# Projections after three graph layers: the normalisation of each pair of tiles moved from VectorE to ScalarE

## The chip, the cores and the metric

The kernel runs on one core of one Trainium2 chip. The metric is the time of one execution on the device in microseconds, the median of several runs. In the text PE is TensorE (matmuls; PEld its weight loads), DVE is VectorE, ACT is ScalarE, POOL is GpSimd and SP is SyncE, which here only issues DMAs.

## The reference

3125 nodes with 128 features and 53125 edges, sorted by destination. Four graph layers follow each other, each added to its input and normalised:

```python
def _layernorm(x, axis=-1, eps=1e-05):
    m = jnp.mean(x, axis=axis, keepdims=True)
    v = jnp.var(x, axis=axis, keepdims=True)
    return (x - m) / jnp.sqrt(v + eps)
...
    x = _layernorm(x + _L0_gnn_ref(x, edge_index, edge_type_16, ...), axis=-1)
    x = _layernorm(x + _L1_gnn_ref(x, src, dst, edge_type_32, ...), axis=-1)
    x = _layernorm(x + _L2_gnn_ref(x, edge_index, L2_gnn_W, L2_gnn_b), axis=-1)
    x = _layernorm(x + _L3_gnn_ref(x, ..., src, dst), axis=-1)
```

The first two layers sum messages of typed edges. The third is `relu(agg @ W.T + b)`, with `agg` the plain sum of the neighbours' rows. The fourth is an attention over the edges with 8 heads, whose queries, keys and values are `x @ Wq + bq` (times 0.25), `x @ Wk + bk` and `x @ Wv + bv`.

## The kernel before, in words

The nodes are 25 tiles of 128 rows. The program has five stages: the three sums over edges (`sums_body` for L[0], L[1] and L[2]), the projections (`post_body` in `sum_layers`), and the attention (`attention`). Each engine runs a stage's instructions in an order written out by hand; between stages all meet (`pass_end`, and `pass_close` on DVE).

The change is in the projections alone. They take the aggregated, transposed rows of the third layer (`aggT`), finish that layer, and make queries, keys and values. The tiles go in pairs: `DUOS` is 13, pair u holds tiles 2u and 2u+1, and the last pair has one tile. For pair u, in the order of the data:

- PE multiplies by the third layer's weights (`last_product`, L970) into `p_g`.
- DVE (`last_front`) adds the bias (L1703), takes relu and adds the layer's input (L1706), and takes mean and variance of each tile (bn_stats L1709, bn_aggr L1713) into `mv`.
- ACT takes the square root of variance plus eps for both tiles in one instruction (`deviations`, L1079) into `std`.
- DVE (`last_back`) takes the reciprocal (L1720) into `rstd` and normalises each tile, `(y - mean) * rstd`, with one tensor_scalar (L1724). The tiles land in `XA`, or in the half of `XH` that a register (`aside`, read by a value_load) names. This raises `s_done`.
- PE transposes both tiles (`last_transposed`, L979), and ACT copies them out of PSUM into `H` (`last_copy`, L1084).
- PE multiplies them by the weights of keys and values (L997); DVE adds the bias (`keys_values`, L1733), and SP stores the result to `kv_d` (L697).

The order on each engine, for u from 0 on: PE does `last_product(u + 1)`, `keys_values(u - 1)`, `last_transposed(u)`, and from u = 3 on one `table_rows` (L987). DVE does `last_front(u)`, `keys_values(u - 2)`, `last_back(u)`, and for u from 1 to 7 one of the `row_tables` (L1674 to L1691). ACT does `deviations(u)`, `last_copy(u)`, then two wipes of the attention's buffers (L1090) and, for u from 3 to 11, one `chunk_tables` (L1097), which reads what `table_rows` made. The wipes and tables are for the attention; nothing in this stage reads them. POOL prepares the tables' input beside the first five pairs or so (L740, L742) and then waits until all keys and values are stored, before it starts the attention's gathers (L1950).

After the last pair PE makes the queries (`queries`, L1007), DVE and ACT split each into three bfloat16 parts (L1741, L1748, L1103), and SP stores them to `q_d` (L700). Then the attention starts.

Of the kernel before, what the change touches and what calls it, by code (L numbers as in the profile page):

```python
# [11 lines left out]
ALU = mybir.AluOpType  # L12
ACT = mybir.ActivationFunctionType
AX_X = mybir.AxisListType.X

P = 128
# [3 lines left out]
NT = 25  # L20
# [290 lines left out]
def sum_layers(nc, ctx, a, d, con, dst_s, base4, n_f, ns_i, np_i, XH, idx, shared, cont, s_arr):  # L311
    def sb(name, shape, dt=F32):
        return ctx.enter_context(nc.sbuf_tensor(name, shape, dt))
# [4 lines left out]
    def sem(name):  # L318
        return ctx.enter_context(nc.semaphore(name))
# [42 lines left out]
    y = sb("y", [P, 4, D])  # L362
    bn6 = sb("bn6", [P, 4, 6])
    mv = sb("mv", [P, 4, 2])
    std = sb("std", [P, 4, 1])
    rstd = sb("rstd", [P, 4, 1])
    kv_s = sb("kv_s", [P, 3, 2, 2 * D])
    work = sb("work", [P, NT * SLAB // 2 + OHS * (KEYS + P) // 2])
    XA, H = XH[:, 0:NT], XH[:, NT:2 * NT]
# [108 lines left out]
    s_y0, s_y, s_bs, s_ba, s_std, s_rs, s_done = (sem(f"s_{k}") for k in ("y0", "y", "bs", "ba", "std", "rs", "done"))  # L478
# [552 lines left out]
    def scalar(act, wiped):  # L1031
        act.dma_start(con[:], a["con"]).then_inc(s_con, 16)
        act.dma_start(lim, a["lim"]).then_inc(s_lim, 16)
        for w, name in ((w_self, "w_self"), (w_bases, "w_bases"), (w_basis, "w_basis"), (w_loop, "w_loop"),
# [7 lines left out]
                       scale=0.0).then_inc(s_clr, 1)  # L1042
# [30 lines left out]
        def deviations(u):  # L1073
            n = min(2, NT - 2 * u)
            two = slice(u % 2 * 2, u % 2 * 2 + n)
            act.wait_ge(s_ba, u + 1)
            if u >= 2:
                act.wait_ge(s_rs, u - 1)
            act.activation(std[:, two, 0], mv[:, two, 1], ACT.Sqrt, bias=con[:, C_EPS:C_EPS + 1], scale=1.0).then_inc(s_std, 1)  # L1079

        def last_copy(u):
            n = min(2, NT - 2 * u)
            act.wait_ge(s_xtr, u + 1)
            act.activation(H[:, 2 * u:2 * u + n, :].rearrange("p t d -> p (t d)"), p_xt[:, 0:n * D],  # L1084
                           ACT.Copy).then_inc(s_xtc, 1)

        def wipe(k):
            for ap in wiped:
                n = ap.shape[1]
                act.activation(ap[:, k * n // DUOS:(k + 1) * n // DUOS],  # L1090
                               bc(con[:, C_ONE:C_ONE + 1], 2, (k + 1) * n // DUOS - k * n // DUOS)[:, 0], ACT.Copy,
                               scale=0.0).then_inc(s_wipe, 1)

        def chunk_tables(n):
            ks = slice(n * TK, min((n + 1) * TK, KB))
            act.wait_ge(s_wide, n + 1)
            act.activation(pen[:, ks], p_o[:, 0:(ks.stop - ks.start) * (P + 1)].rearrange("p (k e) -> p k e", e=P + 1),  # L1097
                           ACT.Copy, scale=LOW).then_inc(s_pen, 1)

        def part(g, k):  # L1100
            tiles = slice(g * QG, min((g + 1) * QG, NT))
            act.wait_ge(s_q[2 * k], g + 1)
            act.activation(q_p[:, tiles, k, :], q_f[:, g % 3, 0:tiles.stop - tiles.start, :],  # L1103
                           ACT.Copy).then_inc(s_q[2 * k + 1], 1)
# [104 lines left out]
        def post_body():  # L1209
            act.wait_ge(s_ball, 32)  # L1210
            act.activation(b_q, b_q, ACT.Copy, scale=float(HD) ** -0.5).then_inc(s_bq, 1)
            for u in range(DUOS):
                deviations(u)
                last_copy(u)
                wipe(u)
                if 0 <= u - 3 < TPARTS:
                    chunk_tables(u - 3)
            for i in range(QGROUPS + 2):
                for k in range(3):
                    if 0 <= i - k < QGROUPS:  # L1220
                        part(i - k, k)
# [3 lines left out]
                       scale=0.0).then_inc(s_clr, 1)  # L1225
# [5 lines left out]
    def vector(dve):  # L1231
# [440 lines left out]
        def row_tables(n):  # L1672
            if n == 0:
                dve.memset(shared[0:1, T_ROW:T_TAB], LOW)  # L1674
                dve.wait_ge(s_rows, 48)
                ins = dve.tensor_tensor(cont[:], bends[:, 0], bends[:, 1], ALU.is_equal)
            elif n == 1:
                ins = dve.tensor_tensor(eq_r[:, 0], ends[:, 0, 0:EC], ends[:, 0, 1:EC + 1], ALU.is_equal)
            elif n == 2:
                ins = dve.tensor_tensor(eq_r[:, 1], ends[:, 1, 0:EC], ends[:, 1, 1:EC + 1], ALU.is_equal)  # L1680
            elif n == 3:
                ins = dve.tensor_tensor(eq_f, ends[:, 1, 0:EC:CB], ends[:, 1, CB:EC + 1:CB], ALU.is_equal)
            elif n == 4:
                dve.wait_ge(s_row, 4)
                ins = dve.tensor_scalar(pen_r[:, :, 0, 1:CB + 1], eq_r[:, 0].rearrange("p (k c) -> p k c", c=CB), -1.0,
                                        -LOW, ALU.add, ALU.mult)
            elif n == 5:
                ins = dve.tensor_scalar(pen_r[:, :, 1, 0:CB], eq_r[:, 1].rearrange("p (k c) -> p k c", c=CB), -1.0,
                                        -LOW, ALU.add, ALU.mult)
            else:  # L1690
                ins = dve.tensor_scalar(pen_f[:, :, 0:KB], bc(eq_f, 1, HEADS), -1.0, -LOW, ALU.add, ALU.mult)  # L1691
            ins.then_inc(s_row, 1)

        def last_front(u):
            if u == 0:
                dve.wait_ge(s_ball, 32)
            n = min(2, NT - 2 * u)
            two = slice(u % 2 * 2, u % 2 * 2 + n)
            tiles = slice(2 * u, 2 * u + n)
            dve.wait_ge(s_o, u + 1)  # L1700
            if u >= 2:
                dve.wait_ge(s_done, u - 1)
            dve.tensor_tensor(y[:, two, :], p_g[:, u % 3, 0:n * D].rearrange("p (t d) -> p t d", d=D), bc(b_lin, 1, n),  # L1703
                              ALU.add).then_inc(s_y0, 1)
            dve.wait_ge(s_y0, u + 1)
            dve.scalar_tensor_tensor(y[:, two, :], y[:, two, :], 0.0, XA[:, tiles, :], ALU.max, ALU.add).then_inc(s_y, 1)  # L1706
            dve.wait_ge(s_y, u + 1)
            for j in range(n):
                last = dve.bn_stats(bn6[:, two.start + j, :], y[:, two.start + j, :])  # L1709
            last.then_inc(s_bs, 1)  # L1710
            dve.wait_ge(s_bs, u + 1)
            for j in range(n):
                last = dve.bn_aggr(mv[:, two.start + j, :], bn6[:, two.start + j, :])  # L1713
            last.then_inc(s_ba, 1)

        def last_back(u, aside):
            n = min(2, NT - 2 * u)
            two = slice(u % 2 * 2, u % 2 * 2 + n)
            dve.wait_ge(s_std, u + 1)
            dve.reciprocal(rstd[:, two, :], std[:, two, :]).then_inc(s_rs, 1)  # L1720
            dve.wait_ge(s_rs, u + 1)
            for j in range(n):
                t, k = 2 * u + j, two.start + j
                last = dve.tensor_scalar(XH[:, t:t + NT + 1, :][:, bass.ds(aside, 1), :].rearrange("p a d -> p (a d)"),  # L1724
                                         y[:, k, :], mv[:, k, 0:1], rstd[:, k, :], ALU.subtract, ALU.mult)
            last.then_inc(s_done, 1)

        def keys_values(u):
            n = min(2, NT - 2 * u)
            dve.wait_ge(s_pkv, u + 1)  # L1730
            if u >= 3:
                dve.wait_ge(s_kvst[u % 3], 16 * (u // 3))
            dve.tensor_tensor(kv_s[:, u % 3, 0:n, :], p_d[:, u % 3, 0:n * 2 * D].rearrange("p (t d) -> p t d", t=n),  # L1733
                              bc(b_kv, 1, n), ALU.add).then_inc(s_kv, 1)
# [9 lines left out]
        def rest(g, k):  # L1744
            n = min(QG, NT - g * QG)
            dve.wait_ge(s_q[2 * k - 1], g + 1)
            part = q_f[:, g % 3, 0:n, :]
            dve.tensor_tensor(part, part, q_p[:, g * QG:g * QG + n, k - 1, :], ALU.subtract).then_inc(s_q[2 * k], 1)  # L1748

        def post_body():  # L1750
            aside = dve.value_load(np_i[0:1, 2:3], min_val=0, max_val=NT)
            for u in range(DUOS + 2):
                if u < DUOS:
                    last_front(u)
                if 0 <= u - 2:
                    keys_values(u - 2)
                if u < DUOS:
                    last_back(u, aside)
                if 1 <= u < 8:
                    row_tables(u - 1)  # L1760
            dve.wait_ge(s_bq, 1)
            for i in range(QGROUPS + 2):
                if i < QGROUPS:
                    scaled(i)
                for k in (1, 2):
                    if 0 <= i - k < QGROUPS:
                        rest(i - k, k)
# [670 lines left out]
```

## Time and profile before

| | us |
|---|---|
| three runs | 2503.83, 2506.83, 2515.24 |
| median | 2506.83 |
| the profiled execution | 2512.79 |
| its span | 2511.0 |

Busy in the span: PE 1715.0 us (68%), PE's weight loads 1376.8 (55%), DVE 1502.9 (60%), POOL 1425.4 (57%), ACT 1127.2 (45%). The granted clock of TensorE has a mean of 0.698 of full speed.

Times in the profile count from the start of the span. A row of the timeline gives the start, the time from the first start to the last end of the instructions in it, the engine, the line, and in brackets how long the engine had been idle and what ended that. Instructions of one engine can overlap a little, so one may start before the one ahead of it ends. The line numbers are those of the kernel before.

### The profile page before, as it was taken

The numbers are of one execution on the slowest core, as the hardware profiler recorded it, in microseconds if no ns is written. First come the engines' busy times: TensorE is split into PE (matmuls) and PEld (weight loads), VectorE is DVE, ScalarE is ACT, GpSimd is POOL, SyncE is SP. The second block draws the span as 40 slices with busy tenths as digits, with TensorE's granted clock in tenths as the row PEclk, the third lists the DMA queues.
The fourth block names the chain that finished last, engine by engine and source line by source line (L and its number), as shares of the span: only waits on it lengthen the run. The fifth ranks groups of instructions, "written<-read, shape, count | busy, mean of one in ns | idle before, by whom it ended". The sixth has DMA issues, their size and how long they took to land.

```text
span 2511.0 us, 36111 instructions
## 1 busy us (share of the span) xinstructions
PE 1715.0 (68%) x10160; PEld 1376.8 (55%) x10160; DVE 1502.9 (60%) x4761; ACT 1127.2 (45%) x2223; POOL 1425.4 (57%) x1482
## 2 busy tenths in 40 slices
PE   2668777777478888884688898986135455564566
PEld 1556656656367666663666666754034454454456
DVE  5556555555467776774366666667345565665666
ACT  2235435545566666664245444534433432433433
POOL 6666666665466666653566666602756455555540
PEclk9655555555688999887789999998555555555555
DMA  5121221212123332323333333312644344443430
GB/s 152 47 75 48 73 74 49 73 48 70 44 80 87 87 114 61 111 81 103 87 87 88 111 90 113 111 64 67 175 133 122 112 132 119 120 130 117 119 114 6
DMA packets 171436, 231.76 MB, mean 92 GB/s; under 512 B 48220, under 2 KB 123983, under 8 KB 170980
## 3 DMA queue, kind: packets, MB, share of 16 engines
q0 software_dynamic: 53376, 123.02, 18.0%
q1 hardware_dynamic: 116710, 104.76, 13.8%
q10 hardware_dynamic: 1154, 1.67, 0.2%
q8 instruction: 86, 1.41, 0.2%
q14 instruction: 110, 0.90, 0.1%
HBM read 196.52 MB, written 36.08 MB: 93 GB/s over the span
## 4 chain that ended last, share of the span: by engine, by line
PE 20%; another core or an unknown queue 16%; ACT 10%; issue 8%; DVE 7%; SPq 2%; DMA 1%; DVEq 0%; ACTq 0%
PE p_d L918 4%; PE p_d L847 4%; PE p_g L905 3%; PE p_g L795 3%; ACT oht L2071 2%; PE p_o L828 1%; ACT oht L2077 1%; PE p_d L807 1%; ACT L2118 1%; PE p_w L2005 1%; ACT late L1122 1%; ACT L2102 1%; DVE Sb L1399 1%; SPq L1915 1%
## 5 line engine op out<-in xcount | busy, mean ns | idle before, releaser
L728 POOL DMA_INDIRECT G<-h_d,idx x624 | 615.9, 987 | 402.1 <-issue 159.4
L1950 POOL DMA_INDIRECT G<-kv_d,idx x416 | 394.5, 948 | 325.1 <-DVE PV L2256 173.8
L728 POOL DMA_INDIRECT G<-in_x,idx x416 | 400.6, 963 | 217.1 <-issue 106.8
L795 PEld LDWEIGHTS p_g<-S,G 128*128 128x128 f32 x2080 | 376.4, 245 | 225.7 <-issue 184.8
L795 PE MATMUL p_g<-S,G 128*128 128x96 f32 (+1 forms) x2080 | 398.3, 325 | 147.4 <-issue 145.2
L1391 DVE TENSOR_TENSOR agg<-agg,p_g 128x96 f32 (+1 forms) x520 | 120.6, 232 | 338.0 <-remote 194.0
L918 PE MATMUL p_d<-Sb,kv_s 128*128 128x288 f32 x728 | 245.1, 458 | 77.4 <-ACT kv_s L1135 57.6
L1482 DVE TENSOR_TENSOR work<-work,p_d 128x312 f32 (+1 forms) x416 | 180.4, 465 | 145.5 <-remote 77.3
L1364 DVE SCALAR_TENSOR_TENSOR S<-con,rel,shared 128x96 f32<-128x96 f32 (+1 forms) x1040 | 262.1, 294 | 0.4 <-issue 0.2
L1143 ACT ACTIVATE work<-con,lo_f 128x128 bf16<-128x128 f32 x416 | 143.1, 392 | 234.0 <-remote 114.8
L807 PE MATMUL p_d<-work 128*128 128x312 bf16 (+1 forms) x832 | 198.6, 368 | 55.1 <-issue 35.0
L2005 PE MATMUL p_w<-oh,PV 128*128 128x40 f32 x832 | 195.1, 410 | 26.0 <-DVE PV L2256 25.1
L2005 PEld LDWEIGHTS p_w<-oh,PV 128*128 128x128 f32 x832 | 187.6, 330 | 33.4 <-DVE PV L2256 28.1
L918 PEld LDWEIGHTS p_d<-Sb,kv_s 128*128 128x128 f32 x728 | 136.7, 210 | 113.8 <-ACT kv_s L1135 62.1
L1399 DVE SCALAR_TENSOR_TENSOR Sb<-con,slots 128x288 f32<-128x288 f32 x364 | 174.3, 513 | 17.2 <-remote 9.4
L1135 ACT ACTIVATE kv_s<-p_g 128x512 f32<-128x512 f32 (+1 forms) x104 | 56.2, 540 | 246.4 <-remote 160.3
L2081 ACT ACTIVATE R<-p_sm 1x128 f32<-1x128 f32 x26 | 6.9, 266 | 328.9 <-remote 306.8
L807 PEld LDWEIGHTS p_d<-work 128*128 128x128 bf16 x832 | 99.9, 134 | 98.5 <-issue 74.2
L1468 DVE TENSOR_SCALAR work<-iota_h,key_f 128x600 bf16<-128x600 f16 x416 | 153.9, 380 | 0.0
L2228 DVE TENSOR_TENSOR_SCAN R<-pen_b,R 1x136 f32<-1x136 f32 x26 | 11.1, 428 | 204.3 <-ACT R L2082 194.6
L847 PE MATMUL p_d<-work,q_s 128*128 128x512 bf16 (+1 forms) x525 | 125.4, 379 | 6.3 <-DMA work<-A_d 4.6
L905 PE MATMUL p_g<-XH,hot 128*128 128x128 f32 x728 | 95.0, 284 | 46.1 <-ACT hot L1128 46.1
(315 smaller groups left out, 3179.5 us busy)
## 6 DMA issues: line engine op xcount, KB each, us to landing
dst_b<-in_dst_row SPq DMA_DIRECT2D x104, 240.0 KB
work<-A_d SPq DMA_DIRECT2D x25, 800.0 KB
A_d<-work SPq DMA_DIRECT2D x12, 1600.0 KB
G<-h_d,idx POOLq DMA_INDIRECT x624
G<-in_x,idx POOLq DMA_INDIRECT x416
kv_s<-low_d SPq DMA_DIRECT2D x52, 128.0 KB
G<-kv_d,idx POOLq DMA_INDIRECT x416
kv_s<-low_d SPq DMA_DIRECT2D x52, 96.0 KB
```

Of the source, the lines that this page charges most:

```text
L728: pool.indirect_dma_start(G[:, n % GRING, :], None, l.table, bass.IndirectOffsetOnAxis(ap=l.places[:, c:c + 1], axis=0)).then_inc(s_arr[i ...
L795: last = pe.matmul(p_g[:, g % PB, 0:width], G[:, c % GRING, :], S[:, c % (SRING * GR), 0:width], start=(k == 0), stop=(k == GR - 1))
L807: last = pe.matmul(p_d[:, 1 + half, 0:(hi - lo) * W], lows[:, slot, :], keys[:, slot, lo * W:hi * W], start=(k == 0), stop=(k == GR - 1))
L847: last = pe.matmul(p_d[:, 1 + n % 2, 0:width], q_s[:, t % QS, k, :], A_s[:, t % AB, cols], start=(t == two[0] and k == 0), stop=(t == two[ ...
L905: last = pe.matmul(p_x[:, k * P:(k + 1) * P], hots[n % 2][:, t % 2, k, :], l.x_in[:, t, :], start=(t == tiles[0]), stop=(t == tiles[-1]))
L918: pe.matmul(p_s[:, 0:l.nb * WB], picked[:, n % 2, at:at + P], Sb[:, m % SBR, 0:l.nb * WB], start=(k == 0), stop=(k == GRP - 1)).then_inc(s ...
L1364: last = dve.scalar_tensor_tensor(S[:, slot + k, 0:l.nb * W].rearrange("p (b w) -> p b w", w=W), bc(iota, 1, l.nb), rel[:, c:c + 1], bc(co ...
L1399: dve.scalar_tensor_tensor(Sb[:, m % SBR, 0:l.nb * WB].rearrange("p (b w) -> p b w", w=WB), bc(con[:, C_I + 1:C_I + 1 + WB], 1, l.nb), row ...
L1468: dve.tensor_scalar(keys[:, slot, :], iota_h[:], key_f[:, c:c + 1], None, ALU.is_equal).then_inc(s_hot, 1)
L1482: dve.tensor_tensor(place, place, p_d[:, 1 + half, 0:(hi - lo) * W].rearrange("p (t w) -> p t w", w=W), ALU.add).then_inc(s_bad, 1)
L1950: pool.indirect_dma_start(G[:, c % KRING, :], None, d["kv"], bass.IndirectOffsetOnAxis(ap=idx[:, c:c + 1], axis=0)).then_inc(s_arr[c // QC ...
L2005: pe.matmul(p_w[:, q % 2, 0:WA], PV[:, q % VRING, c, :], oh1[:, k % OH1, j * QC + c, :], start=(c == 0), stop=(c == QC - 1))
```

## The change: what it does

The tensor_scalar on DVE is replaced by an ACTIVATE (Identity, which gives scale * x + bias) on ACT for each tile, with `rstd` as scale and `shift` as bias, where `shift` is minus mean times `rstd`. DVE makes `shift` for both tiles of a pair with one scalar_tensor_tensor behind the reciprocal. Both raise `s_rs`, so its counts double. The reciprocal, which overwrites what ACT reads as scale, gets a wait on `s_done`. The value_load of `aside` moves from DVE to ACT, behind the scaling of `b_q` (L1211).

```diff
     rstd = sb("rstd", [P, 4, 1])
+    shift = sb("shift", [P, 4, 1])
...
             if u >= 2:
-                act.wait_ge(s_rs, u - 1)
+                act.wait_ge(s_rs, 2 * (u - 1))
             act.activation(std[:, two, 0], mv[:, two, 1], ACT.Sqrt, bias=con[:, C_EPS:C_EPS + 1], scale=1.0).then_inc(s_std, 1)
+
+        def normalised(u, aside):
+            n = min(2, NT - 2 * u)
+            act.wait_ge(s_rs, 2 * (u + 1))
+            for j in range(n):
+                t, k = 2 * u + j, u % 2 * 2 + j
+                last = act.activation(XH[:, t:t + NT + 1, :][:, bass.ds(aside, 1), :].rearrange("p a d -> p (a d)"),
+                                      y[:, k, :], ACT.Identity, bias=shift[:, k, :], scale=rstd[:, k, :])
+            last.then_inc(s_done, 1)
...
             act.activation(b_q, b_q, ACT.Copy, scale=float(HD) ** -0.5).then_inc(s_bq, 1)
+            aside = act.value_load(np_i[0:1, 2:3], min_val=0, max_val=NT)
             for u in range(DUOS):
                 deviations(u)
+                normalised(u, aside)
                 last_copy(u)
...
-        def last_back(u, aside):
+        def last_back(u):
             n = min(2, NT - 2 * u)
             two = slice(u % 2 * 2, u % 2 * 2 + n)
             dve.wait_ge(s_std, u + 1)
+            if u >= 2:
+                dve.wait_ge(s_done, u - 1)
             dve.reciprocal(rstd[:, two, :], std[:, two, :]).then_inc(s_rs, 1)
-            dve.wait_ge(s_rs, u + 1)
-            for j in range(n):
-                t, k = 2 * u + j, two.start + j
-                last = dve.tensor_scalar(XH[:, t:t + NT + 1, :][:, bass.ds(aside, 1), :].rearrange("p a d -> p (a d)"),
-                                         y[:, k, :], mv[:, k, 0:1], rstd[:, k, :], ALU.subtract, ALU.mult)
-            last.then_inc(s_done, 1)
+            dve.wait_ge(s_rs, 2 * u + 1)
+            dve.scalar_tensor_tensor(shift[:, two, 0], mv[:, two, 0], -1.0, rstd[:, two, 0], ALU.mult,
+                                     ALU.mult).then_inc(s_rs, 1)
...
         def post_body():
-            aside = dve.value_load(np_i[0:1, 2:3], min_val=0, max_val=NT)
...
-                    last_back(u, aside)
+                    last_back(u)
```

## Rows read from the trace of the kernel before

**Rows 1.** The head of the page.

```profile
span 2511.0 us, 36111 instructions
```

**Rows 2.** Busy by window: us, PE, PEld, DVE, ACT, POOL, clock, DMA share, GB/s.

```profile
1707.30:1711.20 3.90, 3.29 (x10) 2.39 (x10) 3.25 (x10) 1.46 (x4) 3.69 (x6) 0.50 0.00 0
...
1726.20:1745.60 19.40, 13.08 (x64) 8.30 (x64) 17.44 (x64) 10.55 (x30) 0.00 (x0) 1.00 0.24 83
1745.60:1748.50 2.90, 2.58 (x7) 1.33 (x7) 2.06 (x7) 1.65 (x5) 0.00 (x0) 0.69 0.31 112
```

**Rows 3.** The timeline, pair 9 and the start of pair 10.

```profile
1737.88 0.29 ACT L1079 ACTIVATE std<-mv,con 128x2 f32<-128x2 f32 x1
1738.20 0.17 DVE L1720 RECIPROCAL rstd<-std 128x2 f32<-128x2 f32 x1
1738.51 0.60 DVE L1724 TENSOR_SCALAR XH<-y,mv,rstd 128x128 f32 x2
1739.03 0.42 DVE L1703 TENSOR_TENSOR y<-p_g,late 128x256 f32<-128x256 f32 x1
...
1739.17 0.44 PE L979 MATMUL p_xt<-con,XH 128*128 128x128 f32 x2 [1.02 <-DVE XH L1724]
...
1739.64 0.38 ACT L1084 ACTIVATE XH<-p_xt 128x256 f32<-128x256 f32 x1 [1.48 <-PE p_xt L979]
...
1739.92 0.61 ACT L1090 ACTIVATE agg<-con 128x499 f32<-128x499 f32 x1
...
1740.43 0.41 ACT L1090 ACTIVATE SC<-con 128x256 f32<-128x256 f32 x1
...
1740.74 0.48 ACT L1097 ACTIVATE shared<-p_o 128x387 f32<-128x387 f32 x1
1741.11 0.29 ACT L1079 ACTIVATE std<-mv,con 128x2 f32<-128x2 f32 x1
1741.44 0.17 DVE L1720 RECIPROCAL rstd<-std 128x2 f32<-128x2 f32 x1 [0.15 <-ACT std L1079]
```

**Rows 4.** The timeline, the first three pairs.

```profile
1704.12 0.31 ACT L1211 ACTIVATE late<-late 128x128 f32<-128x128 f32 x1 [27.58 <-DMA late<-in_w_qkv]
...
1705.84 0.30 ACT L1079 ACTIVATE std<-mv,con 128x2 f32<-128x2 f32 x1 [1.41 <-DVE mv L1713]
...
1709.93 1.23 DVE L1724 TENSOR_SCALAR XH<-y,mv,rstd 128x128 f32 x2
...
1711.21 0.69 PE L979 MATMUL p_xt<-con,XH 128*128 128x128 f32 x2 [0.51 <-DVE XH L1724]
1711.33 0.97 DVE L1674 MEMSET shared<- 1x1100 f32 x1 [0.17 <-issue]
...
1714.76 0.98 DVE L1724 TENSOR_SCALAR XH<-y,mv,rstd 128x128 f32 x2
```

**Rows 5.** Groups by line and form: busy us, mean ns, idle before.

```profile
L1167 ACT ACTIVATE hot<-con,kv_s 128x128 f32<-128x128 f32 x208 | 63.3, 386 | 37.7 <-remote 36.3 <-PE p_g L881 1.4
...
L1064 ACT ACTIVATE act_r<-p_o,now 128x128 f32<-128x128 f32 x25 | 9.0, 361 | 0.0
...
L1063 ACT ACTIVATE act_o<-p_o 128x128 f32<-128x128 f32 x25 | 6.9, 277 | 37.1 <-remote 26.1 <-PE p_o L832 7.0 <-issue 3.8
...
L1568 DVE SCALAR_TENSOR_TENSOR now<-now,npf,itc 128x1 f32<-128x1 f32 x2 | 0.4, 200 | 0.0
```

**Rows 6.** Waits from 1750 to 1800 us: us in total, times, longest.

```profile
DVE cur L2165 <- issue: 2.1, 1, 2.1
```

**Rows 7.** The timeline of ACT in the third sum.

```profile
1618.42 1.28 ACT L1070 ACT_TABLE_LOAD   x1
...
1623.79 1.32 ACT L1122 ACTIVATE hot<-kv_s,con 128x512 f32<-128x512 bf16 x2
```

**Rows 8.** The timeline, transposes of the last two pairs.

```profile
1745.64 0.44 PE L979 MATMUL p_xt<-con,XH 128*128 128x128 f32 x2 [1.19 <-DVE XH L1724]
...
1748.51 0.48 PE L979 MATMUL p_xt<-con,XH 128*128 128x128 f32 x1
```

## The prediction

> **What bounds the kernel now.** I read four views in this order. The head of the profile gives the span, 2511.0 us [rows 1]; the same execution took 2512.79 us, so 1.8 us lie around the span, and it stands 6 us above the median of the three runs, 2506.83. The sum below is a difference, so I set it against 2512.79 and carry it over to the median unchanged. The busy time by window shows where the change lives: the projections run from 1704 to about 1751 us, some 47 us or 1.9% of the span, and within 1726.2 to 1745.6 no engine is full: DVE 17.44 of 19.40 us, PE 13.08, ACT 10.55 [rows 2]. No single engine's sum therefore gives the answer; the loop of waits does.
>
> That loop is in the timeline of one steady pair [rows 3]. ACT takes the square root of pair 9 (L1079) at 1737.88, DVE's reciprocal starts at 1738.20, DVE's normalisation at 1738.51, PE's transposes at 1739.17, ACT's copy out of PSUM (L1084) at 1739.64; then ACT does work which nobody in this stage waits for, two wipes (1739.92 and 1740.43) and one table (1740.74), and only then, at 1741.11, the square root of pair 10. That is 3.23 us, and each step starts on the end of the one before it. ACT is idle in it for 1.48 us, but its order is fixed, so the square root of the next pair can't pass the wipes. DVE runs nearly as long: it idles only 0.15 us, at 1741.44, where the reciprocal waits for the square root [rows 3]. So two loops are almost equal, and ACT's is ahead by that 0.15 us.
>
> **The change, part by part.**
>
> Removed from DVE: 25 normalisations. In the steady pairs two of them take 0.60 us and hold DVE's queue 0.52 us (1738.51 to 1739.03) [rows 3]. In the first pairs they cost more: 1.23 us for pair 1 and 0.98 for pair 2 [rows 4], where POOL is busy 3.69 of 3.90 us [rows 2]; from the start of pair 1's to DVE's next instruction 1.40 us go by [rows 4].
>
> Added to DVE: 13 small operations for the bias. The nearest row is a scalar_tensor_tensor on 128x1, 200 ns [rows 5]. The reciprocal's start to its dependant's start is 0.31 us now [rows 3] and stays, with the small operation in the dependant's place. ACT then starts on its end, so 0.20 us is new in the loop. Bounds: 0.16, if it costs what the reciprocal does (0.17 less a rounding), and 0.3.
>
> Added to ACT: 25 ACTIVATEs on 128x128, scale and bias both from SBUF. No row has both. With a pointer for the bias, 128x128 f32 takes 386 ns; a pointer for the scale is worth 361 - 277 = 84 ns, from the two ACTIVATEs on the same PSUM tile [rows 5]. I take 470 ns. Consecutive ACTIVATEs overlap by 0.10 us (1739.92 + 0.61 against 1740.43) [rows 3], so a pair takes 0.94 - 0.10 = 0.84 us, against 0.60 on DVE: 0.24 us more in the loop. Bounds: 0.07, if the second pointer is free (2 x 386 - 100 = 672 ns), and 0.34 with no overlap. The output's address comes from a register, as it did on DVE, and I see no gap for it there: I price it at nothing.
>
> Moved in the queues: on ACT the normalisation stands between square root and copy. What waits behind it is this pair's copy, which needs the transposes of this very data anyway, then wipes, table and the next square root. So nothing can use ACT's wait for DVE's two small operations, as nothing could before. On DVE, the next front (L1703) and the keys and values (L1733) now start as soon as the bias is out, 0.52 us sooner; they end earlier and DVE waits for the square root instead. The added wait on s_done before the reciprocal is for a normalisation two pairs back, long over. DMAs are neither added nor moved.
>
> So a steady pair gets 0.20 + 0.24 = 0.44 us longer, 3.23 to 3.67. The steps stay alike to the end: from pair 9's transposes at 1739.17 [rows 3] to pair 11's at 1745.64 [rows 8] it is 6.47 us for two. From the transposes of pair 4 to those of pair 11 there are seven such steps: **+3.1 us**. The last pair has one tile: + 0.20 and 0.47 against 0.35: **+0.3 us**.
>
> The first four pairs go the other way. There ACT has no table to do (0.30 us less), and DVE has a memset of 0.97 us [rows 4] and row tables on top, so DVE is the late one at pairs 2 and 3. Walking these pairs with the durations above (normalisation gone from DVE, bias added, 0.84 us on ACT) gives, as an estimate, the transposes of pairs 0 to 4 at +0.2, +0.1, -0.4, -0.5 and -0.2 us against now; ACT's loop catches up as soon as its tables begin. I take **-0.2 us** for the lot, with bounds of -1.5 (all of DVE's relief stays) and +0.5.
>
> The value_load moved to ACT sits between the scaling of b_q and the first square root. The only bound from a row is DVE's 2.1 us of issue ahead of L2165, where a value_load and more stand [rows 6]. ACT has 1.4 us between these two now (1704.12 + 0.31 to 1705.84) [rows 4], so it costs 0 to 0.7 us once; I take 0.1.
>
> What follows the stage starts from its end: the queries, which PE has in its queue behind the last keys and values, the 25 stores of q, and the attention, which reads what they store; POOL's gathers wait for the last store of keys and values. I take the delay as passed on whole; nothing ahead of the attention has slack to swallow it, though a loop as long as the attention's could give or take a little.
>
> Sum: 3.1 + 0.3 - 0.2 + 0.1 = **+3.3 us**. The profiled execution would be 2516.1, the median 2510.1 us. About 0.5% (12.5 us) is what a measurement can tell from no change here, and this is a quarter of it.
>
> **The clock, weighed.** From 1719.4 to 1745.6 the granted clock is 1.00, the 2.4 GHz level, with PE busy 67% of the time; in the first pairs it is 0.50, the 1.2 GHz level, and it falls again after 1745.6, to a mean of 0.69 [rows 2]. In my sum it stays at 1.00. The Trainium skill, TensorE: Matmul & The Clock Gate, Part 1, says that the clock follows how busy PE has been recently; with pairs of 3.67 us the same work is 59% of the time, so by that rule the fall may come sooner. That is the first rival.
>
> **Rivals.**
>
> 1. *The clock falls within the steady pairs.* The transposes of a pair took 0.69 us at 0.50 (pair 1) and 0.44 at 1.00 [rows 3, 4]. So 0.25 us for some eight pairs: 2.0 us more, +5.3 in all, 2512.1. For it: the fall after 1745.6 came at no great loss of activity. Against: the stretch before held for 26 us. 15%.
>
> 2. *DVE was the loop that counted, and ACT's is shorter than I think.* If the wipes overlapped the waits, only DVE's relief would remain: 0.52 - 0.20 = 0.32 us per pair, times 13: -4.2 us, 2502.6. It decides at whether the square root of the next pair starts on the end of L1097 or earlier; the rows show it on the end, 1740.74 and 1741.11 [rows 3]. 9%.
>
> 3. *Slower: tables are loaded again.* ACT has one function more in this stage. If Identity needed another set than Sqrt, each of the 13 pairs would load twice at 1.28 us, in the very loop: 33 us, less the 0.3 or so hidden in the wait for DVE, per pair: about 29, so 2539. It decides at the first pair. Against: after the load for Sqrt at 1618.42, Square at 1623.79 needs none [rows 7], and Sqrt and Copy alternate in this stage with none. The Trainium skill, ScalarE: Activation LUTs, section on table sets, says that cheap functions, identity among them, are in every set; no run here has shown Identity. 3%.
>
> 4. *The rest of the program shifts.* Instructions move from DVE's stream to ACT's and the attention starts in another phase; nothing in the trace gives this a sign. The three runs span 2503.83 to 2515.24, and I allow the same: 5 us either way, with a small chance of over 12. 13%.
>
> **How the numbers follow.** My forecast has 60%, the rivals 15, 9, 3 and 13. The range reaches from the second rival less a little of the spread of the runs, 2501, over the low bound of the sum (0.23 us per pair for seven steps, less 1.5: about +0.3, 2507) and the high bound (0.64 per pair, with +0.5 and 0.7: about +6, 2513) to the first rival with its spread, 2519. Over 0.5% faster means below 2494.3: only rival 4 gets there, 2%. Slower means above 2519.4: rival 3 and a part of 1 and 4, 6%. The rest, 92%, is no change.
>
> **What would show each step.** In the profile of the changed kernel: the two ACTIVATEs of a pair at 0.84 us together, some 470 ns each, in the place of 0.60 us on DVE; the small operation at some 200 ns, and 0.20 us from its start to ACT's; transposes 3.67 us apart in the pairs with tables; DVE waiting about 0.8 us per pair for the square root; ACT still going straight from wipes and table into it; no ACT_TABLE_LOAD between 1704 and 1755; the last transpose at about 1751.8 in place of 1748.51 [rows 8]. Wrong would be: steps of 3.2 us or less (rival 2), transposes of 0.69 us in the steady pairs (rival 1), or a difference at the end that is far from the difference at the last transpose (rival 4).

## The result, and the profile after

The changed kernel takes 2521.99 us (median of 22 runs, 2514.25 to 2531.56), the kernel before 2515.15 us (22 runs, 2503.83 to 2525.86). The ratio is 1.0024, interval 1.0013 to 1.0036: 6.0 us slower, between 3.3 and 9.1 (the two medians are 6.8 us apart). The interval leaves out 1, so the change does make the kernel slower, by less than the 0.5% that the prediction counts as a change. The prediction had 2510.1 us and the range 2501 to 2519: the forecast difference of +3.3 us is at the interval's low end, and the measured time lies 3.0 us above the range. The two misses have different causes, and the larger one isn't the change: the 22 runs of the kernel before have a median 8.3 us above that of the three which the prediction had (2506.83).

The span is 2522.8 us, from this head of the page of the changed kernel:

```profile
span 2522.8 us, 36135 instructions
```

The first operation of the projections starts at 1711.45, against 1704.12 [rows 4]. These 7.3 us come from the stages ahead, whose code the change doesn't touch; the experiments show how much they vary. So times below that are compared between traces are counted from this operation, the first L1703 (L1715 in the changed kernel). The timeline of the changed kernel, one steady pair (pair 6), answers to [rows 3]:

```profile
1736.28 0.29 ACT L1080 ACTIVATE std<-mv,con 128x2 f32<-128x2 f32 x1
1736.60 0.17 DVE L1734 RECIPROCAL rstd<-std 128x2 f32<-128x2 f32 x1 [0.88 <-ACT std L1080]
1736.80 0.16 DVE L1736 SCALAR_TENSOR_TENSOR shift<-mv,rstd 128x2 f32<-128x2 f32 x1
...
1737.09 0.88 ACT L1087 ACTIVATE XH<-y,shift,rstd 128x128 f32 x2 [0.52 <-DVE shift L1736]
...
1738.02 0.44 PE L980 MATMUL p_xt<-con,XH 128*128 128x128 f32 x2 [1.48 <-ACT XH L1087]
...
1738.50 0.38 ACT L1094 ACTIVATE XH<-p_xt 128x256 f32<-128x256 f32 x1 [0.53 <-PE p_xt L980]
...
1738.78 0.61 ACT L1100 ACTIVATE agg<-con 128x499 f32<-128x499 f32 x1
...
1739.29 0.41 ACT L1100 ACTIVATE SC<-con 128x256 f32<-128x256 f32 x1
1739.59 0.48 ACT L1107 ACTIVATE shared<-p_o 128x387 f32<-128x387 f32 x1
1739.97 0.29 ACT L1080 ACTIVATE std<-mv,con 128x2 f32<-128x2 f32 x1
```

From square root to square root it is 3.69 us, where it was 3.23. ACT still goes from wipes and table straight into the next square root. DVE's idle time has grown: the reciprocal now waits 0.88 us for it. That is DVE's relief, and nothing uses it. The waits of DVE in the stage, first of the changed kernel (us in total, times, longest):

```profile
DVE rstd L1734 <- ACT std L1080: 12.2, 12, 1.7
```

and of the kernel before:

```profile
DVE rstd L1720 <- ACT std L1079: 1.6, 5, 0.5
```

DVE gives 10.6 us back as waiting. More rows of the changed kernel matter: a group of ACT, two stretches by window (columns as in [rows 2]), and the transposes of a pair in the second stretch:

```profile
L1087 ACT ACTIVATE XH<-y,shift,rstd 128x128 f32 x25 | 11.0, 485 | 8.3 <-DVE shift L1736 8.3
```

```profile
1727.00:1745.00 18.00, 11.40 (x55) 7.10 (x55) 12.94 (x50) 12.84 (x35) 0.00 (x0) 0.96 0.21 73
1745.00:1749.50 4.50, 4.10 (x12) 2.58 (x13) 2.94 (x12) 2.98 (x8) 0.00 (x0) 0.50 0.17 58
```

```profile
1745.40 0.69 PE L980 MATMUL p_xt<-con,XH 128*128 128x128 f32 x2 [1.10 <-ACT XH L1087]
```

The ACTIVATE with both pointers takes 485 ns (470 forecast). And the granted clock falls to 0.50, the 1.2 GHz level, in the middle of the steady pairs. In the 18 us up to 1745, PE was busy 63% of the time (11.40 of 18.00), against 67% where the clock held in the kernel before [rows 2]. The pair's transposes take 0.69 us there, 0.44 at 1.00.

The stage in one table, worked out from the timelines: "transposes" is from the first DVE operation to the last transposes (L979, L980), "attention" from the first DVE operation to SP's first load of the attention (`dst_b`), "remaining" from there to the end of the span. The experiments are described below. The usual step is that of the late pairs.

| kernel | starts at | transposes | attention | remaining | usual step |
|---|---|---|---|---|---|
| before | 1704.12 | 44.39 | 77.74 | 729.1 | 3.23 |
| changed | 1711.45 | 48.89 | 81.86 | 729.5 | 3.69 |
| e0_before | 1701.55 | 44.65 | 77.83 | 727.5 | 3.24 |
| e1_after | 1702.90 | 47.51 | 81.59 | 726.9 | 3.68 |
| e8_after_again | 1699.42 | 49.09 | 81.97 | 728.6 | 3.69 |
| e2_after_wipes | 1703.34 | 40.13 | 70.93 | 733.9 | 2.87 |
| e9_wipes_again | 1701.46 | 39.98 | 70.14 | 731.8 | 2.87 |
| e3_before_wipes | 1709.25 | 43.13 | 74.71 | 732.2 | 2.99 |
| e4_bias_only | 1710.90 | 48.68 | 81.80 | 729.8 | 3.43 |
| e5_pe_busy | 1702.20 | 48.43 | 81.21 | 733.0 | 3.69 |
| e6_pool_late | 1707.99 | 47.73 | 79.32 | 732.8 | 3.69 |
| e7_split | 1711.41 | 44.72 | 79.52 | 731.4 | 3.30 |

### The profile page after: what moved, and what is told of

Same layout as the page of the kernel before. It is cut to its first block, busy times and chain, and to the rows that moved or that the text cites. A ratio compares the mean times of both kernels' runs of the same rounds, so it can differ in the third digit from the quotient of the medians.

```text
span 2522.8 us, 36135 instructions
## 1 busy us (share of the span) xinstructions
PE 1718.9 (68%) x10160; PEld 1375.3 (55%) x10160; DVE 1498.0 (59%) x4749; ACT 1139.5 (45%) x2248; POOL 1420.9 (56%) x1482
## 4 chain that ended last, share of the span: by engine, by line
PE 38%; another core or an unknown queue 21%; issue 15%; ACT 15%; DVE 8%; SPq 2%; DVEq 1%; DMA 1%; ACTq 0%
PE p_g L796 9%; PE p_d L919 5%; PE p_d L808 5%; PE p_g L906 4%; PE p_d L848 4%; PE p_o L829 2%; ACT oht L2081 2%; PE p_g L889 1%; ACT work L1153 1%; ACT oht L2087 1%; PE p_g L882 1%; ACT late L1132 1%; DVE S L1376 1%; ACT work L1166 1%
```

## The experiments

In the expectations, theory A is that ACT's loop sets the pace and that the stage holds the whole difference; theory B is that more is lost outside the stage. Ratios are against runs of the kernel before that were taken beside each experiment. e4, e5 and e6 have one run each (2524.33, 2518.22 and 2521.90 us): they are read by their traces alone, and their whole times say nothing.

**The same two kernels again.** e0_before is the kernel before and e1_after and e8_after_again are the changed kernel, with no edit.

> The kernel before once more, for a second trace of it. If the 7.3 us by which the changed kernel's projections began later (1711.45 against 1704.12) are variation of the stages ahead, this trace begins its projections anywhere between 1700 and 1716 us, with the stage itself unchanged: 44.4 us from the first DVE operation (L1703) to the last transposes (L979), steps of 3.23 us. If the change had done it, this one begins near 1704 again. Ratio 1.000.

Measured: ratio 1.0008 (0.9992 to 1.0024); the projections start at 1701.55, and the stage is as before, 44.65 us to the last transposes with steps of 3.24.

> The changed kernel once more. Theory A (ACT's loop sets the pace): 48 to 49 us from the first DVE operation to the last transposes, 4.0 to 4.5 over before, steps of 3.69 us, 3.93 where the clock is at the 1.2 GHz level; ratio 1.0018. Theory B (something outside the stage adds the rest of the 6 us): the start of the projections is late by some 2 us or more against the kernel before also in this pair of traces, ratio 1.0024 or more.

Measured: ratio 1.0022 (1.0007 to 1.0038), start at 1702.90, 47.51 us to the last transposes, 0.5 under the forecast. The start is 1.35 us later than in e0_before, and the ratio lies between those of the two theories, so this pair alone doesn't decide between them.

> The changed kernel a third time, for the whole time and a third trace. Theory A: stage from its first DVE operation to the attention's first load 81.2 to 81.9 us against 77.8 before, so 3.4 to 4.1 us more; ratio 1.0015, interval holding 1.0014 to 1.0016. Theory B (more is lost outside the stage): ratio 1.0022 or above once more.

Measured: ratio 1.0015 (0.9995 to 1.0035), start at 1699.42, the stage 81.97 us, just above the forecast 81.9. The start of the projections, behind code that is the same everywhere, lies anywhere from 1699.42 to 1711.45 in the table, and the changed kernel holds both ends. So the 7.3 us of the first pair of traces are variation. The stage up to the attention is 81.6 to 82.0 us in the changed kernel and 77.7 and 77.8 before: **+4.0 us**. That is 1.0016, which all three intervals hold. For theory B, a further loss outside the stage, the measured ratios leave up to some 5 us, and none shows that it exists.

**The order on ACT.** e2_after_wipes puts one wipe into each of ACT's two waits:

```diff
-        def wipe(k):
-            for ap in wiped:
+        def wipe(k, which=(0, 1)):
+            for ap in [wiped[w] for w in which]:
...
                 deviations(u)
+                if u > 0:
+                    wipe(u - 1, (0,))
                 normalised(u, aside)
+                if u > 0:
+                    wipe(u - 1, (1,))
                 last_copy(u)
-                wipe(u)
                 if 0 <= u - 3 < TPARTS:
                     chunk_tables(u - 3)
+            wipe(DUOS - 1)
```

> The changed kernel with one wipe in each of ACT's two waits: the wipes of the pair before, one between square root and normalisation, one between normalisation and copy. Theory A: 0.8 us leave ACT's loop, steps fall from 3.69 to about 2.9 (DVE's own loop), 3.0 to 3.3 where DVE has a row table; the stage is some 7 us shorter than in the changed kernel and 3 shorter than before, ratio 0.9985. Rival (DVE or PE sets the pace, ACT's order is no matter): steps stay at 3.69, ratio as for the changed kernel.

> The changed kernel with the wipes in ACT's waits, again. If the 6.9 us that the stage lost against before arrive at the end, ratio 0.9973; if the attention gives some back because it starts sooner, ratio 0.9986 again, and the stretch from the attention's first load to the end is some 3 us longer than in the trace of the changed kernel of this same call.

e9_wipes_again is the same kernel as e2_after_wipes. Its timeline, ACT alone, from one square root to the next:

```profile
1734.43 0.30 ACT L1080 ACTIVATE std<-mv,con 128x2 f32<-128x2 f32 x1
1734.62 0.61 ACT L1100 ACTIVATE agg<-con 128x499 f32<-128x499 f32 x1
1735.25 0.88 ACT L1087 ACTIVATE XH<-y,shift,rstd 128x128 f32 x2
1736.03 0.40 ACT L1100 ACTIVATE SC<-con 128x256 f32<-128x256 f32 x1
1736.65 0.38 ACT L1094 ACTIVATE XH<-p_xt 128x256 f32<-128x256 f32 x1 [0.22 <-PE p_xt L980]
1736.93 0.49 ACT L1107 ACTIVATE shared<-p_o 128x387 f32<-128x387 f32 x1
1737.31 0.29 ACT L1080 ACTIVATE std<-mv,con 128x2 f32<-128x2 f32 x1
```

The same work in another order, and a step of 2.88 us in place of 3.69: 0.8 us were the two wipes on the path. This settles that ACT's loop set the pace. Ratios: 0.9986 (0.9969 to 1.0003) for e2 and 0.9970 (0.9955 to 0.9985) for e9, the latter 7.5 us faster than before. Both times this version is faster than the changed kernel measured beside it (medians 2510.29 against 2517.81, 2508.37 against 2520.23). That it also beats the kernel before is shown by e9 alone: e2's interval holds 1. Of e9's two forecasts the ratio fits the first (0.9973), and the stretch behind the attention's first load the second: it is 3.2 us longer than in e8 (731.8 against 728.6).

Of the 7.6 us by which e9's stage is shorter than before, 4.4 lie ahead of the last transposes and 3.2 behind them. In this order the clock doesn't fall at the stage's end. By window (columns as above), the 10 us from about the last transposes on, of the kernel before and of e9_wipes_again:

```profile
1748.50:1758.50 10.00, 8.54 (x51) 7.88 (x51) 5.66 (x10) 4.77 (x9) 3.24 (x4) 0.75 0.25 81
```

```profile
1741.40:1751.40 10.00, 6.88 (x53) 6.25 (x53) 6.76 (x12) 6.87 (x13) 3.88 (x4) 0.98 0.33 101
```

and in it 48 of the queries' matmuls, before and in e9:

```profile
1750.37 7.05 PE L1007 MATMUL p_d<-late,XH 128*128 128x128 f32 x48
```

```profile
1742.67 5.52 PE L1008 MATMUL p_d<-late,XH 128*128 128x128 f32 x48
```

These 48 take 5.52 us in e2, e9 and e3, the three traces in which the clock stays at 1.00 through them, and 6.34 to 7.83 us in the other nine, in all of which it is at 0.50 for a part. Up to the first store of q, 9.2 us behind the last transposes before and 7.0 in e9, this gives 2.2 of the 3.2 us. The last 1.0 can't be put down to anything: from that store to the attention's first load the twelve traces take between 22.5 and 25.6 us.

**The same order in the kernel before.** e3_before_wipes puts both wipes between square root and copy, where ACT waits in a steady pair of that kernel [rows 3].

```diff
                 deviations(u)
+                if u > 0:
+                    wipe(u - 1)
                 last_copy(u)
-                wipe(u)
                 if 0 <= u - 3 < TPARTS:
                     chunk_tables(u - 3)
+            wipe(DUOS - 1)
```

> The kernel before with its two wipes put between square root and copy, where ACT waits 1.48 us. Theory A with two nearly equal loops: only the 0.15 us by which ACT's loop was ahead is won, steps of 3.08 where they were 3.23, the stage 1 us shorter, ratio 0.9995. If ACT's loop alone counted and DVE had room, steps would fall to 2.5.

Measured: ratio 0.9986 (0.9971 to 1.0000), the last transposes at 43.13 us. DVE's timeline shows the other loop, now the bound:

```profile
1745.62 0.66 DVE L1735 TENSOR_TENSOR kv_s<-p_d,late 128x512 f32<-128x512 f32 x1
1746.20 0.16 DVE L1722 RECIPROCAL rstd<-std 128x2 f32<-128x2 f32 x1
1746.50 0.60 DVE L1726 TENSOR_SCALAR XH<-y,mv,rstd 128x128 f32 x2
```

The reciprocal no longer waits for anything. Steps are 2.99 us (pairs with row tables up to 3.27), so 0.24 us shorter and not 0.15; what the other 0.09 is, no run shows. Here the stage wins 1.3 us to the last transposes and 3.0 to the attention. With the wipes in ACT's waits the change is worth another 0.12 us per step (2.87 in e2), whereas with the old order it costs 0.46. So in the steps it depends on ACT's order whether DVE's relief pays, with the same work on each engine. The whole time doesn't show the gain: e2 and e3 both have the ratio 0.9986.

**The small operation alone.** e4_bias_only adds it to the kernel before and leaves the normalisation on DVE:

```diff
+    shift = sb("shift", [P, 4, 1])
...
-                act.wait_ge(s_rs, u - 1)
+                act.wait_ge(s_rs, 2 * (u - 1))
...
-            dve.wait_ge(s_rs, u + 1)
+            dve.wait_ge(s_rs, 2 * u + 1)
+            dve.scalar_tensor_tensor(shift[:, two, 0], mv[:, two, 0], -1.0, rstd[:, two, 0], ALU.mult,
+                                     ALU.mult).then_inc(s_rs, 1)
+            dve.wait_ge(s_rs, 2 * u + 2)
             for j in range(n):
...
-                                         y[:, k, :], mv[:, k, 0:1], rstd[:, k, :], ALU.subtract, ALU.mult)
+                                         y[:, k, :], rstd[:, k, :], shift[:, k, :], ALU.mult, ALU.add)
```

> The kernel before with only the small bias operation added behind the reciprocal; both normalisations stay on DVE (y * rstd + shift). Theory A: 0.20 us more in the loop, steps from 3.23 to 3.43 us, the last transposes at about 46.8 us from the stage's start. If the small operation costs nothing in the loop, steps stay at 3.23.

Measured: steps of 3.43 us, so 0.20 us as forecast. But the last transposes come at 48.68 us, 1.9 later than expected. 1.5 of that is there at pair 4, behind the pairs beside which POOL works: 21.34 us, where 18.82 before and 0.20 for each of five pairs would give 19.8. Two things in that stretch can be read off the trace: the small operation takes 0.73, 0.46 and 0.57 us in pairs 0 to 2 and 0.16 after, which is 1.3 us more, and the transposes of pairs 3 and 4 take 0.69 and 0.63 us, at the low clock.

**The clock.** e5_pe_busy does PE's product for the next pair twice.

```diff
-            for j in range(min(2, NT - 2 * u)):
+            for j in [j for _ in range(2) for j in range(min(2, NT - 2 * u))]:
                 t = 2 * u + j
                 last = pe.matmul(p_g[:, u % 3, j * D:(j + 1) * D], aggT[:, t * P:(t + 1) * P], w_lin[:], start=True,
```

> The changed kernel with PE's products for the next pair done twice (same values), so that PE is busy 0.7 us more per pair. If the steps of 3.93 us are the clock's fall and nothing else, all transposes from pair 2 on take 0.44 us and all steps with tables 3.68 or 3.69. If they have another cause, some steps of 3.93 remain at a granted clock of 1.00.

Measured, by window:

```profile
1727.00:1745.00 18.00, 12.86 (x74) 8.89 (x73) 12.53 (x47) 12.76 (x35) 0.00 (x0) 1.00 0.21 75
```

PE is busy 71% of the time (some 0.3 us more per pair, not 0.7), the clock stays at 1.00, and all steps with tables are 3.68 or 3.69 us. The changed kernel has steps of 3.93 or 3.94 in each of its three traces, always behind steady pairs whose transposes take 0.69 us (8 and 9, then 4 in e1, 7 and 8 in e8); e7_split has one such step (3.55 for 3.30, behind pair 4). So the long steps are the clock's fall, which costs 0.25 us per step, 0.25 to 0.5 us in each of the three traces. That the additional work kept the clock up isn't shown by this one trace: in e6_pool_late (below), with steps of 3.69 and no additional work, it stays at 1.00 through the steady pairs too.

**POOL.** e6_pool_late holds POOL's table work back until pair 2 is normalised.

```diff
             pool.wait_ge(s_dT, 16)
+            pool.wait_ge(s_done, 3)
             for n in range(TPARTS):
```

> The changed kernel with POOL's table work held back until pair 2 is normalised. If POOL's work is what stretches the bias operation to 0.53 to 0.80 us, the bias operations of pairs 0 to 2 take 0.16 us, and pair 2's transposes come at about 10.9 us from the stage's start in place of 12.21; the long ones, if any, move to the pairs that now stand beside POOL. Rival (they are long because the stage's first instructions are): no change, 0.5 us or more in pairs 0 to 2.

Measured: 0.16 us in pairs 0 to 2, pair 2's transposes at 10.64 us (12.21 in the changed kernel), and the long one moves to pair 3. DVE and POOL of e6_pool_late, beside each other:

```profile
1717.41 0.16 DVE L1737 SCALAR_TENSOR_TENSOR shift<-mv,rstd 128x2 f32<-128x2 f32 x1
...
1720.72 0.80 DVE L1737 SCALAR_TENSOR_TENSOR shift<-mv,rstd 128x2 f32<-128x2 f32 x1
```

```profile
1720.67 0.82 POOL L744 TENSOR_TENSOR agg<-agg 16x387 bf16<-16x387 f32 x1
```

The DVE operation on two elements per partition starts 0.05 us behind POOL's and ends with it, at 1721.5. The changed kernel shows the same in pair 1, 0.80 us from 1717.63, beside POOL's 0.82 us from 1717.59. So this small operation costs beside POOL what is left of the POOL operation that it meets. The Trainium skill, SBUF — State Buffer, section "SBUF: two separate sides", says that DVE and GpSimd share a pair of ports as a lock held for a whole instruction, and that a DVE operation with two SBUF inputs takes part in it against a GpSimd operation that reads SBUF. This trace agrees, with 0.80 us for 0.16.

**Half and half.** e7_split normalises the first tile of a pair on DVE and the second on ACT.

```diff
-            for j in range(n):
+            for j in range(n - 1, n):
                 t, k = 2 * u + j, u % 2 * 2 + j
                 last = act.activation(XH[:, t:t + NT + 1, :][:, bass.ds(aside, 1), :].rearrange("p a d -> p (a d)"),
...
+            if n == 2:
+                t, k = 2 * u, two.start
+                dve.tensor_scalar(XH[:, t:t + NT + 1, :][:, bass.ds(aside, 1), :].rearrange("p a d -> p (a d)"),
+                                  y[:, k, :], mv[:, k, 0:1], rstd[:, k, :], ALU.subtract, ALU.mult).then_inc(s_tanh, 1)
...
             pe.wait_ge(s_done, u + 1)
+            if u < DUOS - 1:
+                pe.wait_ge(s_tanh, u + 1)
```

> The changed kernel with the first tile of each pair normalised by DVE and the second by ACT, side by side. Theory A: 0.39 us of ACT's 0.88 leave the loop, steps of 3.30 us against 3.69 changed and 3.23 before; DVE stays under it (about 3.0). The whole is then the time of before within what can be told, ratio 1.000 to 1.001. If something outside the stage made the changed kernel slower, its ratio stays at 1.002.

Measured: steps of 3.30 us, the last transposes at 44.72 us (44.39 before), ratio 0.9997 (0.9980 to 1.0014). As expected in the loop, and in the ratio. The stretch to the attention was 79.52 us, 1.7 to 1.8 above before, of which 0.3 is there at the last transposes. The first store of q comes 9.2 us behind them, as before; the rest lies behind that store, where e7 has the longest stretch of the twelve traces (25.6 us; 24.1 and 24.5 before).

## Why the prediction was right or wrong

**The loop was read rightly.** Forecast 3.67 us per step, measured 3.69. From the reciprocal's start to the normalisation's it is 0.49 us (1736.60 to 1737.09) against 0.31, so 0.18 for the small operation (forecast 0.20; e4 0.20), and from there to the transposes 0.93 against 0.66, so 0.27 for the two ACTIVATEs (forecast 0.24). The three things looked for were there: DVE waits 0.88 us, ACT goes straight on, no table is loaded in the stage. The wait added on s_done and the value_load cost nothing: the first square root comes 1.72 us behind the first DVE operation in both kernels (1713.17 - 1711.45; [rows 4]).

**Rival 2, DVE as the loop that counts, fell.** DVE lost work and got waiting in its place. Its decision point, where the next square root starts, was the right one to look at; e2 moved that point, and each step got 0.8 us shorter.

**Rival 3 and rival 4.** No table is loaded, so rival 3 fell. Rival 4's sign appeared in the first pair of traces, whose spans differ by 11.8 us: 7.3 of it stands ahead of the projections, and e0, e1 and e8 show it to be scatter and not the change.

**Rival 1, the clock, came true in part.** Its sign, transposes of 0.69 us in the steady pairs, was there in all three traces of the changed kernel, for one or two pairs and not eight: +0.25 to +0.5 us, plus about 0.2 at pair 11 in two of them. It should have been a term of the sum at this size instead of a rival at 2.0. On this point the rule of the Trainium skill (TensorE: Matmul & The Clock Gate, Part 1), that the clock follows how busy PE has been recently, was nearer than the sum. With less work per time the clock went down in these three traces and in neither of the kernel before. But e6 held it with the same work, so how often it falls at this pace stays open.

**The terms that mis-sized the difference.** Over three traces of the changed kernel and two of the kernel before, the difference at the attention's first load is +4.0 us, where +3.3 was forecast. The seven steps are the forecast +3.1. The largest gap is the clock, which the sum had at nothing: +0.4. The last pair is +0.5 for +0.3: 0.20 for the small operation, 0.49 for 0.35, and its predecessor at the low clock in two traces. The first pairs ("for the lot -0.2 us") come to 0.0 on the mean, and the value_load's +0.1 to nothing.

That mean of the first pairs hides the least certain term. Against the first trace of the kernel before, pair 4's transposes came 0.38 us late in the first trace and 0.51 late in e8, but 0.54 us early in e1, where the bias operations met POOL less (0.16, 0.21 and 0.57 us, against 0.53, 0.80 and 0.58). The walk took the small operation at 0.20 us everywhere, although [rows 4] showed DVE operations stretched beside POOL. What was taken off DVE there came back on a smaller operation with the same wait. So in the first trace this term was the largest gap: +0.4 (first pairs), +3.1 (seven steps), +0.5 (clock), +0.5 (last pair) is +4.5 at the last transposes, 48.89 us from the stage's start, where 47.7 was forecast (1751.8 - 1704.12).

**The step that failed** is "I set it against 2512.79 and carry it over to the median unchanged", with rival 4's "5 us either way". The three runs contained the two lowest of all 22, 2503.83 and 2506.83, and their median was 8.3 us too low as an anchor. That was bad luck of the draw and no drift: the runs of the kernel before beside the experiments have medians of 2514.52, 2515.80 and 2515.98 us. The profiled execution, at 2512.79, said as much: it lay 6 us above a median from three values that themselves spread over 11 us, and I chose the median alone. Against the 22 runs the same sum gives 2518.5, and the measured 2521.99 is 3.5 us above. The width was wrong with it: the bounds took the scatter around the anchor, and none for the anchor itself. "No change", at 92%, came out by the prediction's own bound of 0.5%. As a statement of what can be told this bound was too coarse: 22 runs of each kernel put the ratio between 1.0013 and 1.0036.

**What stays open.** The remaining time behind the attention's first load varies from 726.9 to 733.9 us, with the same code. It is 731.8 and 733.9 in the two traces of the reordered kernel and 726.9 to 729.5 in those of the changed one and of the one before, but also 733.0 in e5, whose stage is about as long as the changed kernel's, and 732.8 in e6. Some of what e2 wins may be given back there: its two ratios, 0.9986 and 0.9970, stand for 3.5 and 7.5 us, the stage for 6.9 and 7.6. Two traces can't tell; no experiment held the attention fixed. What sets the 22.5 to 25.6 us between the first store of q and the attention's first load is open too.

## What to carry to other kernels

Where each engine runs an order written by hand, follow one item through the engines and back to the start of the next. Where that loop is the longest and passes through the engine that you add work to, relief on the other engine buys nothing, and what stands in the loop without being wanted there (here the wipes) is what to move first. The same edit cost 0.46 us per step in one order of ACT and gained 0.12 in another. And when the effect is a quarter of what the runs scatter, forecast the difference, count the profiled run among the runs, and give the time a wider range than three runs span.

## What the runs showed of the hardware that I had not expected

- A DVE operation on 128x2 with two inputs from SBUF takes 0.16 us alone and up to 0.80 us when it begins behind a POOL tensor_tensor of 0.82 us; it ends with POOL's. The ACTIVATEs beside the same POOL work took their 0.88 us for two, as everywhere.
- An ACTIVATE on 128x128 f32 with scale and bias both from SBUF takes 485 ns; with the bias alone it was 386 [rows 5].
- The granted clock fell within the changed kernel's steady pairs in all three of its traces, for one or two pairs, and in neither trace of the kernel before. Reordering ACT's wipes shortened the queries on PE, 7.05 to 5.52 us for 48 matmuls: the clock then stayed at 1.00 through them (e2, e9, e3).
- Twelve traces with the same code ahead of the projections start them between 1699.4 and 1711.5 us.
